# Graph network kernel: counts matrix from one-hot products on TensorE, in units of 64 targets

## What is computed

```python
p1 = tanh(p @ pp_W1 + pp_b1) @ pp_W2 + pp_b2
inter = concatenate([p1[src], p1[dst]]) @ pi_W1 + pi_b1
inter = (inter @ pi_W2 + pi_b2) @ pi_W3               # [edges, 64, 8]
i1 = einsum('ecb,eb->ec', inter, edge_attr_8)
i1 = tanh(i1 @ ii_W1 + ii_b1) @ ii_W2 + ii_b2
x = x + segment_sum(i1, dst)
# then 7 times, with different scales and weights:
agg = segment_sum(h[src], dst)
```

## Time and profile before

| | |
|---|---|
| median of the runs | 9151.09 us |
| the profiled execution: span | 9166.2 us |
| busy PE, DVE, ACT, POOL | 7037.3, 2225.1, 656.9, 3763.7 us |
| HBM read, written | 1741.08 MB, 173.66 MB |

### The profile page before, as it was taken

The page is one execution under the profiler, slowest core; times in us unless marked ns, Lnnn a source line. Parts: engine busy times, 40 slices in busy tenths (PEclk is TensorE's granted clock), DMA queues, the critical chain, the costliest instruction groups (busy, mean ns, idle before and its releaser), DMA issues. The chain is left out here.

```text
span 9166.2 us, 122664 instructions
## 1 busy us (share of the span) xinstructions
PE 7037.3 (77%) x41928; PEld 4791.7 (52%) x41928; DVE 2225.1 (24%) x1980; ACT 656.9 (7%) x1115; POOL 3763.7 (41%) x3477
## 2 busy tenths in 40 slices
PE   3156666666666666666666799999999999999999
PEld 2145555555555555555555555555555555555554
DVE  8633333233333333333332400000111000011000
ACT  2100000000000000000000000000000000000000
POOL 1177777778777787777777100000000000000000
PEclk9577777777777777777777799999999999999999
DMA  9966666565666656666566588888788888888877
GB/s 363 409 142 138 135 137 135 135 143 131 137 140 140 139 132 137 139 139 135 133 140 139 143 277 273 270 274 276 266 273 280 291 290 285 291 287 294 274 258 239
DMA packets 693574, 1916.47 MB, mean 209 GB/s; under 512 B 168266, under 2 KB 221866, under 8 KB 680938
## 3 DMA queue, kind: packets, MB, share of 16 engines
q1 hardware_dynamic: 577738, 1653.85, 62.9%
q0 software_dynamic: 114720, 261.05, 9.2%
q10 hardware_dynamic: 1024, 0.26, 0.0%
HBM read 1741.08 MB, written 173.66 MB: 209 GB/s over the span
## 5 line engine op out<-in xcount | busy, mean ns | idle before, releaser
L1127 PE MATMUL ps_a<-ring,table 128*128 128x448 fp8e4 x19208 | 3661.1, 353 | 52.8 <-DVE table L103 31.0
L1127 PEld LDWEIGHTS ps_a<-ring,table 128*128 128x128 f16 x19208 | 1882.3, 98 | 1807.7 <-issue 82.7
L698 PE MATMUL ps_u<-from_node,window 128*128 128x512 f32 x788 | 711.3, 1002 | 1792.4 <-DMA gathered<-u_source,plan_now 1494.8
L538 POOL DMA_INDIRECT counts<-plan_now x1568 | 1806.5, 1152 | 451.0 <-issue 430.6
L523 POOL DMA_INDIRECT gathered<-u_source,plan_now x1576 | 1736.7, 1102 | 480.9 <-issue 479.6
L920 POOL COPY hst<-h 128x896 f32 x28 | 26.7, 954 | 3915.7 <-PE ps_t L1142 2484.8
L714 PE MATMUL ps_m<-M_sb,z 128*128 128x64 f32 x12544 | 1422.3, 274 | 0.0
L714 PEld LDWEIGHTS ps_m<-M_sb,z 128*128 128x128 f32 x12544 | 1416.5, 192 | 0.0
L698 PEld LDWEIGHTS ps_u<-from_node,window 128*128 128x128 f32 x788 | 198.7, 311 | 1833.9 <-issue 1833.9
L629 DVE TENSOR_TENSOR z<-u,basis 128x2048 f32<-128x2048 f32 x392 | 878.4, 2281 | 0.0
L700 PEld LDWEIGHTS ps_u<-ident,gathered 128*128 128x128 f32 x3152 | 616.4, 271 | 361.7 <-issue 361.7
(11 more groups left out here) (158 smaller groups left out, 2296.4 us busy)
## 6 DMA issues: line engine op xcount, KB each, us to landing
ring<-counts SPq DMA_DIRECT2D x2401, 448.0 KB, 4.2
basis<-in_basisT SPq DMA_DIRECT2D x394, 1024.0 KB
counts<-zero POOLq DMA_DIRECT2D x98, 1568.0 KB, 7.0
dst_all<-in_dst_seq SPq DMA_DIRECT2D x197, 512.0 KB
gathered<-u_source,plan_now POOLq DMA_INDIRECT x1576
counts<-plan_now POOLq DMA_INDIRECT x1568
window<-u_target SPq DMA_DIRECT2D x197, 64.0 KB
u_source<-us SPq DMA_DIRECT2D x7, 896.0 KB
```

Of the source, the lines that this page charges most:

```text
L538: pool.indirect_dma_start(A_cells, bass.IndirectOffsetOnAxis(ap=plan[q][:, ET + i:ET + i + 1], axis=0), plan[q][:, 2 * ET:PLAN].bitcast(U8 ...
L698: mm(ps_u[h][:, :], window[q][:, :], from_node[q][:, 512 * h:512 * h + 512], start=True, stop=False)
L1127: last = mm(ps_a[:, b, 0:BC], table[n % 2][:, KC * k + i, :], ring[k % SLOTS][:, i, BC * b:BC * b + BC].bitcast(F8), start=(k == 0 and i = ...
```

## The change

- The zero fill, the byte addresses, the 49 shifts and the scatters go. The counts matrix is laid out in 196 units of 64 targets, `[unit, partition, source tile, target]`.
- `prepare` finds for each of 2548 blocks of 5 targets (13 to a unit) where its edges begin: 20 scans over the 1568 first targets of the tiles, 20 indirect gathers of whole rows, a count, and 20 gathers of the 128 edges from there on. From them it makes two codes for each edge, `cell` (source tile times 5 plus target) and `lane` (source mod 128), and turns them with 40 transposes so that edges lie on partitions. The codes are 16-bit.
- In `edges` DVE writes one-hots of them, 13 `cell_hot` of 490 columns and one `lane_hot` of 13 times 128 columns a group, PE multiplies them (13 products of 490 columns into two PSUM banks in turn), ACT copies each result as fp8 into `unit` and SP stores the unit, 784 KB, in the counts matrix. `z` is made from `ps_u` in PSUM, without ACT's copy; its bias is folded into the tables. POOL's loop is written out in full and only gathers.
- `basis[1]` and `z[1]` take the place of `x_sb`, which `after_edges` loads again.
- `dense` reads the counts bank by bank, in 12 chunks a group (4 banks, tiles 0 to 32, 33 to 65, 66 to 97) through 3 slots, in runs of 2112 or 2048 bytes; a product reads 7 runs of 64 bytes a partition.

```diff
-            with pool.Fori(0, A_BYTES // P // width // 2 - 1) as i:
-                for q in range(2):
-                    pool.wait_ge(zeroed[q], 16 * i + 16)
-                    fill(i + 1, q)
+            for q in range(BQ):
+                pool.indirect_dma_start(rec[:, q, :], None, rows, bass.IndirectOffsetOnAxis(ap=row_of[:, q:q + 1], axis=0)).then_inc(S["chunk"], 16)
+            pool.wait_ge(S["rec_at"], 1)
+            for q in range(BQ):
+                pool.indirect_dma_start(rec[:, q, :], None, records, bass.IndirectOffsetOnAxis(ap=at[:, q:q + 1], axis=0)).then_inc(S["rec"], 16)
...
+            for q in range(BQ):
+                ch(nc.vector.tensor_scalar(below, samples[:, :], first[:, q:q + 1], 0.0, ALU.is_lt, ALU.add, accum_out=found[:, q:q + 1]))
...
+            near_by = KW - REACH
+            for s in range(1, REACH + 1):
+                ch(nc.vector.tensor_tensor(t1[:, 0:near_by], t2[:, 0:near_by], t2[:, s:s + near_by], ALU.bitwise_xor))
...
-                for u in range(SHIFTS // GROUPS):
-                    s = g * (SHIFTS // GROUPS) + (u + 1)
...
 # edges, ACT
+                def empty(t, q, blocks):
...
+                        nc.scalar.copy(unit[q][:, :, BD * i:BD * i + n], got[:, :, 0:n], saturate=False).then_inc(S["emptied"], 1)
 # edges, DVE
+                def place_lanes(t, q):
+                    dve.wait_ge(S["counted"], UB * g)
...
+                def place_cells(t, q, blocks):
+                    for i in blocks:
+                        user = (g, i - RING) if i >= RING else (g - 1, i + RING if i + RING < UB else i)
+                        dve.wait_ge(S["counted"], multiplied(*user))
+                        nc.vector.tensor_scalar(cell_hot[i % RING][:, :], T["iota_n"][:, :], T["cell"][:, bass.ds(g * UB + i, 1)], None, ALU.is_equal).then_inc(S["cells"], 1)
...
+                        place_to(t, q)
+                        place_cells(t, q, range(0, 11))
+                        for h in multiply(*following):
+                            if h == 0:
+                                dve.wait_ge(S["m_done"], 4 * t + 2 * q + 4)
+                                nc.vector.tensor_tensor(msg[q][:, :, 0:D], ps_m[q][:, :, :], T["iib1"][:, :].unsqueeze(1).to_broadcast([P, ET, D]), ALU.add).then_inc(S[f"m_bias{q}"], 1)
+                        place_from(t + 1, q)
+                        place_cells(t, q, range(11, UB))
+                        place_lanes(*following)
                         add(g)
 # edges, PE
+                def count(g, q, blocks):
+                    for i in blocks:
+                        if i == 0:
+                            pe.wait_ge(S["lanes"], g + 1)
+                        pe.wait_ge(S["cells"], written(g, i))
+                        pe.wait_ge(S["emptied"], taken_out(g, i) - 2)
+                        mm(ps_c[(UB * q + i) % 2][:, 0:TILES * BD], lane_hot[q][:, i, :], cell_hot[i % RING][:, :], start=True, stop=True).then_inc(S["counted"], 1)
...
-                        join(*((t, 1) if q == 0 else (t + 1, 0)))
+                        for h in join(*((t, 1) if q == 0 else (t + 1, 0))):
+                            count(g, q, ([0], [1, 2])[h])
...
+                                if 4 * h + i < 7:
+                                    count(g, q, [3 + 4 * h + i])
+                        count(g, q, [10])
                         sum_group(1 - q, t + q, g)
+                        count(g, q, [11, 12])
 # dense, PE
+                for j in chunks:
+                    (k0, k1), b, s = PARTS[j // BANKS], j % BANKS, j % SLOTS
+                    pe.wait_ge(a_in[s], 16 * (CHUNKS // SLOTS * G_ + (j // SLOTS + 1)))
...
+                    for k in range(k0, k1):
+                        if first and b == 0 and (k % GT == 0 or k == k0):
+                            pe.wait_ge(S["input"], GROUPS * n + k // GT + 1)
+                        cells = ring[:, s, :, k - k0, :].bitcast(F8)
```

More of the change, by code:

```diff
@@ L136, in build, with prepare @@
             esb = lambda n, s, d: edge.enter_context(nc.sbuf_tensor(n, s, d))
[L138 to L143, removed]
-            T["aggT"] = esb("aggT", [D + 1, NP + W], F32)
[L145 to L151, removed]
+            T["plan"] = esb("plan", [P, ETILES + ET], I32)
+            T["dloc"] = esb("dloc", [P, ETILES], F32)
+            T["cell"] = esb("cell", [P, BQ * P], F16)
+            T["lane"] = esb("lane", [P, BQ * P + UB], F16)
+            T["iota_n"] = esb("iota_n", [P, TILES * BD], F16)
+            prepare(nc, T, x, w, Us, Ud, irregular)
+            T["aggT"] = esb("aggT", [D + 1, NP + W], F32)
+            edges(nc, T, A_units, Us, Ud, w, G)
+            after_edges(nc, T, x, w)
+        dense(nc, T, A_units, w, out, G)
+def prepare(nc, T, x, w, Us, Ud, irregular):
     with ExitStack() as c:
@@ new lines, in _ @@
+            ch(nc.vector.tensor_reduce(out=faults[:, 2:3], in_=pairs_seen[:, 0:near_by], op=ALU.add, axis=AX.X))
+            ch(nc.vector.tensor_scalar(faults[:, 2:3], faults[:, 2:3], 8.5, None, ALU.is_gt))
+            dve.wait_ge(S["chunk"], 16 * BQ)
+            lines = [P, BQ, P]
+            ends = rec[:, :, :].rearrange("p q (e h) -> p q e h", h=2)
+            start_of = first[:, :].unsqueeze(2).to_broadcast(lines)
+            ch(nc.vector.tensor_tensor(near[:, :, :], ends[:, :, :, 1], start_of, ALU.is_lt))
@@ L435, in edges @@
         gathered = two(sb, "gathered", [P, ET, 2 * D], F32)
-        u = two(sb, "u", [P, 512], F32)
-        z = two(sb, "z", [P, 4, 512], F32)
         msg = two(sb, "msg", [P, ET, D + 1], F32)
-        plan = two(sb, "plan_now", [P, PLAN], I32)
+        lane_hot = two(sb, "lane_hot", [P, UB, P], F16)
+        cell_hot = [sb(f"cell_hot{i}", [P, TILES * BD], F16) for i in range(RING)]
+        unit = two(sb, "unit", [P, TILES, UC], F8)
         ps_u = two(ps, "ps_u", [P, 512])
@@ L701, in join @@
                         last.then_inc(S[f"u{q}"], 1)
-                join(0, 0)
+                        yield h
+                for h in join(0, 0):
+                    pass
                 with pe.Fori(0, STEPS) as t:
@@ L808, with dense @@
 NORMS = [2, 5]
-def dense(nc, T, A_blocks, w, out, G):
+def dense(nc, T, A_units, w, out, G):
     with ExitStack() as c:
@@ L1198, in group @@
                 with pe.If(flag < 1):
-                    for segment in range(3, CHUNKS // SLOTS):
-                        blocks(n, G_, segment, first)
+                    blocks(n, G_, range(3, CHUNKS), first)
                 with pe.Else():
```

547 lines of the change are left out of this document (290 added, 257 removed).

## The result

The changed kernel takes 8056.03 us (median of 4 runs, 8042.87 to 8063.05) where the kernel before, timed beside it, takes 9153.74 (4 runs, 9141.64 to 9167.48): a ratio of 0.8795, with a 95% interval of 0.8783 to 0.8808. That is faster, as forecast, and 159 us less than the 8215 forecast. The profiled execution has a span of 8052.8 us.

What follows compares the result with a forecast made beforehand. The prediction took POOL's instruction stream to bound edges. From the span, 9166 - 203 (prepare) - 768 (edges) + 15 (after_edges) + 20 (dense) = 8230; with the median 15 us below the span, 8215 us, range 7950 to 8850.

Steps and rivals of the forecast that it cites:

- The bound: In edges POOL's stream was the bound, 4475 of 4635 us; after the change the order, with DMA next at 16 us.
- prepare: First stage: ends at about 260 us instead of 463 as the zero fill goes, -203 us (bounds -240 and -170).
- edges: 196 turns of 19.5 us and 45 us at the ends, 3867 against 4635: -768 us; turn bounds 15.7 and 22.5.
- The loop through count 0: In edges: 11.2 us on PE from count 0, then 8.4 on DVE to cell 0, forecast as 19.5 us a group.
- The ends of the stage: In edges: 45 us beside the 196 turns.
- The waits: In edges: PE waits some 2 us in two places, ahead of counts 11 and 0, released by DVE's cells.
- after_edges: Stage after edges: x_sb is loaded again ahead of the weights on the same queue, +15 us.
- dense: Last stage: products unchanged and transfers fast enough, 0 us; one stall at its start, +20 us.
- (a): Rival in edges: DVE's chain overlaps better and the turn falls to PE's own length, 16.5 us: 7627 us; chance 0.08.
- (b): Rival in edges: PE's waits bring its clock down, 22.5 us a turn: 8803 us; chance 0.17.
- (c): Rival in edges: POOL stays the bound, gathers stretched beside DVE's one-hots, 23.2 us a group: 8940 us; chance 0.05.
- (d): Rival in dense: DMA becomes the bound since runs are shorter, at 215 GB/s 9345 us, slower; chance 0.04.

Runs made afterwards that it cites:

- r2: The changed kernel with lane_hot of the next group written right after cell 10 instead of after cell 12: 7887.65 us, ratio 0.8599.
- s1: r4_all with the loads of dst_all and window put ahead of those of basis, with semaphores of their own: 7609.2 us, ratio 0.8309.
- t1: s1 with the store of a unit put ahead of the load before it on SP's queue: ratio 0.8272 in four of six runs.
- t2: t1 with half of each basis load left out after the first two groups, for its time alone: 7399.51 us, ratio 0.8081.
- b3_z_from_sbuf: The changed kernel with u copied by ACT from PSUM to SBUF and z multiplied from there: 8092.42 us, ratio 0.8824.
- r4_all: The changed kernel with to_node and lane_hot put after cell 10, and from_node and cells 11 and 12 ahead of the second z: 8031.91 us, ratio 0.8761.
- the four edited kernels: The changed kernel with DVE's order edited: cells 11 and 12 earlier, lane_hot earlier, to_node later, or all rearranged: ratios 0.8451, 0.7983, 0.8145 and 0.7509.

## Why the prediction was right, point by point

**The bound.** POOL's stream was the bound of `edges`, and with the scatters gone POOL idles. The forecast that the order sets the turn, and that DMA is next behind it, held: r2 and s1 show the first, t1 and t2 the second. The DMA engines' need is 0.83 of 18.73, 15.5 us a turn, where 16 was set.

**prepare.** -213 us against -203: the first gather of `edges` starts at 250.2, not 265. The node loop (138 us from the first square root at 101.8 to the last copy at 239.3, 148 forecast) began 12 us late, and the transposes, copies and the flag behind it took 11 us instead of 20.

**edges, the term that was mis-sized.** 18.73 us a turn instead of 19.5 is 151 us, nearly all of the miss. The loop through count 0 itself was 1.2 us shorter than forecast: 18.3 in the turns in which it binds. PE's part was 10.7 instead of 11.2 (count products and `z` products overlap at their ends, which I added up in full), three cells came at 0.29 instead of 0.41 and `from_node` at 0.74 instead of 0.81; the rest, some 0.3 us, had been set for hand-overs and the branch. I had scaled the cell from an operation with 32-bit input, and that price alone was 0.4 us a turn, some 70 us. The perf-mode tier table of the Trainium skill (VectorE: DVE Perf Modes), which I weighed and didn't take, gives four elements a cycle, by its figures an estimate of 0.29 us. The trace agrees nearly: 0.285 us of busy time a cell, 0.26 in a row, 0.34 for one alone. Every second turn then took 19.2 us, because of the slow join products, and brought the mean up to 18.73. The sum had no term for that; so 0.4 us a turn, some 80 us, of the nearness of 8215 to 8056 is luck: a cost left out made up for part of one set too high.

The ends of the stage took 64 us (3735 - 196 x 18.73) where 45 were set. Against the span the terms give -10 (prepare), -151 (turns), +19 (ends), +2 and -37 (dense), together -177 (8230 to 8052.8); the median then lay 3 us above the span and not 15 below, hence 159.

**The waits.** PE was to idle some 2 us ahead of counts 11 and 0. It idles 2.04 ahead of count 11 in every turn and 0.84 ahead of count 0 in every second. What the prediction missed is that these are two loops of nearly one length. The one through count 0 takes 18.3 us; the one through count 11 takes 17.5 with the join at the upper level of the clock (10.7 us on PE, 4.0 on DVE from `msg` to count 11, 2.8 on PE up to count 0) and 19.2 with slow join products, when it is the longer. So mending either alone gives little. Why the join is slow in every second turn only, behind the same wait, no run shows.

**after_edges.** +17 us against +15, PE's first product waiting 19.3 us for weights that are queued behind `x_sb`.

**dense.** -17 us against +20, the only term of the wrong sign. The stall was there and cost some 17 us; what failed was the step "products unchanged, 0 us", since the kernel before had nine short waits, 20.7 us in all, that I had not listed. Products stayed at 189 ns (326 in 61.83 us, from 4115.76 on).

**The rivals.** (a) PE alone: 15.5 us is real, but needs three orders mended and less traffic. (b) The lower clock after a 2 us wait: it occurs, in the join alone, in every second turn and makes it 0.9 us longer; the mean clock is 0.95, not 0.79. (c) POOL: its mechanism is real, as b3_z_from_sbuf shows, and the change itself took it away by leaving `u` in PSUM. For the cells it doesn't hold: 388 gathers of the changed kernel overlap cells, and none of them lasts over 0.96 us (two rows of the turn before the one above). The rule that the prediction took from the Trainium skill (SBUF — State Buffer, SBUF: two separate sides), that DVE's two-port modes keep GpSimd off a shared port pair, would have let the cells starve the gathers as well; the measurement decides against it. What stretched them was `z` with both operands in SBUF, which the same section names beside those modes, against a GpSimd instruction that reads SBUF; there the trace agrees.

```profile
2516.35 0.94 POOL L559 DMA_INDIRECT gathered<-u_source,plan  x1 [0.30 <-issue]
...
2516.44 0.35 DVE L640 TENSOR_SCALAR cell_hot<-iota_n,cell 128x490 f16<-128x490 f16 x1 [0.64 <-PE ps_c L731]
```

(d) DMA in `dense`: 277 GB/s at a share of 0.79, transfers landing after 7.1 us; no wait for the ring:

```profile
ring<-counts SPq DMA_DIRECT2D x140, 1848.0 KB, 7.1
ring<-counts SPq DMA_DIRECT2D x70, 1792.0 KB, 7.0
```

## What to carry to other kernels

When two engines hand work to and fro and none is busy over 85%, write down every closed loop (PE, DVE and each transfer between its release and its use) with its length; the turn is the longest, and mending one gives only the distance to the next. A loop's length can also change from turn to turn, with PE's clock: look at several turns, not one. Before moving a consumer earlier, look which part of a load it waits for: one semaphore over a large and a small transfer makes the small one as late as the large. The order of instructions on DVE and two loads put ahead of the large ones were worth 5.4% here (ratio 0.8309 against 0.8779) with the same arithmetic.

## What the runs showed of the hardware that was not expected

A gather's time on POOL depends on where DVE's operands lie: 0.94 us beside `z` with one operand in PSUM, up to 2.55 beside the same `z` with both in SBUF. It isn't slowed in proportion but held: wherever it begins within the DVE instruction, it ends 0.81 to 0.83 us after that instruction's end (all 390 of them in b3_z_from_sbuf). In r4_all the same is seen at `to_node` and `lane_hot` (both operands in SBUF, the latter of 16 bits), which ran until 2500.96 and from 2500.87 to 2502.76:

```profile
2500.64 1.14 POOL L559 DMA_INDIRECT gathered<-u_source,plan  x1 [0.30 <-issue]
2502.08 1.50 POOL L559 DMA_INDIRECT gathered<-u_source,plan  x1 [0.30 <-issue]
```

The first gather ends 0.82 us after `to_node`, the second 0.82 us after `lane_hot`. A gather that began before such an instruction kept 0.94 us in nearly all cases (389 in b3_z_from_sbuf, median 0.94).

One chip ran `edges` of the four edited kernels slower, with idle time on three engines that the profile puts down to `issue` or `remote`, while `dense` ran at the usual pace. The kernel before took 1.8 ms longer there; where, no trace shows.
